# Unpaired last lags of a mixed-scale convolution: one stacked stationary and a 64-row product in place of two 128-row products

## The reference

```
x = x + L0(_gn(x), ...)      # mixture of experts: 8 experts, top 2
x = x + L1(_gn(x), ...)      # three layers of this kind, L1 to L3
x = x + L2(_gn(x), ...)
x = x + L3(_gn(x), ...)

def _L1_conv_ref(x, w3, w7, w15, w_mix):          # 4 batches, 512 tokens, 16 heads of 32
    x_flat = x.reshape(b, l, h * d).transpose(0, 2, 1)
    outs = [_causal_dwconv(x_flat, w) for w in (w3, w7, w15)]   # causal, one filter per channel
    y = jnp.concatenate(outs, axis=1)
    y = y.reshape(b, h, n_scales * d, l).transpose(0, 3, 1, 2)
    return jnp.einsum('blhm,dm->blhd', y, w_mix)
```

## Time and profile before

| | us |
|---|---|
| median of 3 runs (1032.67 to 1033.59) | 1032.7 |
| the profiled execution, whole | 1034.63 |
| its span, first to last instruction | 1033.0 |
| PE busy in the span | 992.5 (96%) |
| DVE busy | 498.2 (48%) |
| ACT busy | 323.2 (31%) |
| POOL busy | 255.8 (25%) |

### The profile page before, as it was taken

How to read it: one execution, slowest core, us unless ns; L and a number is a source line. 1 busy time by engine, 2 the same in 40 slices (tenths; PEclk the granted TensorE clock), 3 DMA queues, 4 the chain that set the end, 5 groups by cost and what they waited for, 6 DMA issues and landing times.

```text
span 1033.0 us, 14467 instructions
## 1 busy us (share of the span) xinstructions
PE 992.5 (96%) x5077; PEld 829.1 (80%) x5078; DVE 498.2 (48%) x660; ACT 323.2 (31%) x437; POOL 255.8 (25%) x359
## 2 busy tenths in 40 slices
PE   4989999999999999999999999968999999999998
PEld 3568888888888888888887888857988898889787
DVE  6763263145136246116337155146733896489411
ACT  2613252144144144125235244122511222122223
POOL 1011112121112112111212111112534245424531
PEclk9999999999999999999999999998999999999999
DMA  9576118934971994981893994975467747674668
GB/s 371 234 263 206 22 30 334 392 107 180 393 259 28 397 393 128 409 303 28 335 389 129 396 376 138 406 222 169 143 204 169 219 143 203 165 223 144 192 152 226
DMA packets 98786, 238.12 MB, mean 231 GB/s; under 512 B 10048, under 2 KB 64576, under 8 KB 83840
## 3 DMA queue, kind: packets, MB, share of 16 engines
q1 hardware_dynamic: 90528, 214.54, 57.6%
q0 software_dynamic: 8080, 23.07, 9.5%
q10 hardware_dynamic: 144, 0.07, 0.0%
HBM read 129.91 MB, written 111.94 MB: 234 GB/s over the span
## 4 chain that ended last, share of the span: by engine, by line
PE 75%; DMA 8%; DVE 6%; issue 5%; SPq 4%; ACT 1%; POOL 0%; ACTq 0%; DVEq 0%; POOLq 0%
PE gate_ps L1020 15%; PE up_ps L1020 15%; PE y_ps L1007 10%; PE head_ps L1598 6%; PE head_ps L1594 6%; PE head_ps L1595 6%; PE y_ps L1010 5%; DMA w_raw<-in_w13T 4%; PE hT_ps L1032 2%; SPq L460 2%; DMA ring<-filters 1%; PE xT_ps L997 1%; DMA rowed<-acc 1%; PE head_ps L1613 1%; PE head_ps L1614 1%
## 5 line engine op out<-in xcount | busy, mean ns | idle before, releaser
L1020 PE MATMUL gate_ps<-front 128*128 128x512 f32 x560 | 176.4, 396 | 2.2 <-DVE xT_lo L867 1.5
L1020 PE MATMUL up_ps<-front 128*128 128x512 f32 x560 | 173.2, 390 | 0.0
L1594 PE MATMUL head_ps<-split,ring 128*128 128x256 f32 (+1 forms) x459 | 158.9, 346 | 4.0 <-DMA ring<-filters 2.4
L1598 PE MATMUL head_ps<-split,ring 128*128 128x256 f32 (+1 forms) x459 | 155.3, 338 | 2.2 <-DVE split L1396 2.2
L1595 PE MATMUL head_ps<-split,ring 128*128 128x256 f32 (+1 forms) x459 | 153.8, 335 | 0.0
L882 DVE TENSOR_TENSOR hidden<-silu,up_ps 128x1024 f32<-128x1024 f32 x35 | 42.7, 1221 | 228.7 <-ACT silu L641 228.7
L1020 PEld LDWEIGHTS up_ps<-front 128*128 128x128 f32 x560 | 105.4, 188 | 22.3
L1020 PEld LDWEIGHTS gate_ps<-front 128*128 128x128 f32 x560 | 102.6, 189 | 22.8 <-DVE front L831 1.8
L528 POOL DMA_INDIRECT acc<-y_row,put x35 | 67.4, 1927 | 214.4 <-ACT y_row L629 214.4
L641 ACT ACTIVATE silu<-gate_ps 128x1024 f32<-128x1024 f32 x35 | 35.9, 1024 | 267.5 <-PE up_ps L1020 267.5
L1007 PE MATMUL y_ps<-w_hi,hT_hi 128*128 128x512 f32 x280 | 112.2, 401 | 1.2 <-ACT hT_hi L623 1.2
(11 more groups left out here) (198 smaller groups left out, 1435.1 us busy)
## 6 DMA issues: line engine op xcount, KB each, us to landing
filters<-rows SPq DMA_DIRECT2D x56, 1568.0 KB
w_raw<-in_w13T SPq DMA_DIRECT2D x32, 1024.0 KB, 16.4
ring<-filters SPq DMA_DIRECT2D x15, 1536.0 KB, 6.6
w_raw<-in_w2T SPq DMA_DIRECT2D x16, 1024.0 KB, 6.0
ring<-filters SPq DMA_DIRECT2D x144, 64.0 KB, 4.1
ring<-filters SPq DMA_DIRECT2D x12, 768.0 KB, 4.8
ring<-filters SPq DMA_DIRECT2D x15, 384.0 KB, 3.7
ring<-filters SPq DMA_DIRECT2D x9, 512.0 KB, 4.0
```

The costliest lines, as they stand in the source:

```text
L1020: last = nc.tensor.matmul(o[:, n, :], a[:, k, :], b[:, k, t, n * 512:(n + 1) * 512], start=(k == 0 and a is xT_hi and b is w13_hi), stop=( ...
L1594: nc.tensor.matmul(place, kernel_hi, x_hi, start=(u == 0 and a == 0), stop=False)
L1598: nc.tensor.matmul(place, kernel_hi, x_lo, start=False, stop=False)
```

## The change

The parts are stored and stacked the other way round, and the unpaired unit is computed from one stacked stationary matrix:

- `filter_sb` has the low part at index 0 and the high part at index 1, and so has DRAM. `at_block` moves by `LAGS` elements so that it lies over the half that is not cleared.
- The unpaired unit's filters come by one transfer: low in rows 0 to 63, high in rows 64 to 127. Three transfers become one. The two transfers of the paired windows now carry one part each for both units, 128 rows of 512 bytes instead of 64 rows of two parts.
- `single` holds x high in both halves; `tail` waits for `high_ok` only.
- PE computes high filter by low x as a product of 64 rows (64 to 127) straight from `split`, behind a wait for `low_ok`, and then one 128-row product of the stacked matrix with `single`. Two matmuls remain two.

```diff
@@ RING_COUNT
-    RING_COUNT.append((_l + 1) * (len(head_runs(_h)) + 5))
+    RING_COUNT.append((_l + 1) * (len(head_runs(_h)) + 3))
@@ experts_part
-        at_block = late_rows[:, 0:TOP_K * TILES * COLUMNS].rearrange(...)
+        at_block = late_rows[:, LAGS:LAGS + TOP_K * TILES * COLUMNS].rearrange(...)
-                        nc.scalar.activation(filter_sb[:, i, 0].bitcast(f32r), filter_sb[:, i, 1], ACT.Copy)...
+                        nc.scalar.activation(filter_sb[:, i, 1].bitcast(f32r), filter_sb[:, i, 0], ACT.Copy)...
-                    nc.vector.tensor_tensor(filter_sb[:, i, 1].bitcast(f32r), filter_sb[:, i, 1], filter_sb[:, i, 0],
+                    nc.vector.tensor_tensor(filter_sb[:, i, 0].bitcast(f32r), filter_sb[:, i, 0], filter_sb[:, i, 1],
                                             ALU.subtract).then_inc(filter_ok, 1)
@@ load_filters
-                for half, m in zip((1, 0), head_shared(h)):
-                    s, j, count = head_parts(h)[m]
-                    begin = SCALE_AT[s] + count * P
-                    sp.dma_start(ring[half * P // 2:(half + 1) * P // 2, at:at + 2 * P].bitcast(f32).rearrange("p (a n) -> p a n", n=P),
-                                 filter_rows[P // 2:P, 2 * (l * GROUPS + j):2 * (l * GROUPS + j + 1), begin:begin + P]).then_inc(ring_in[h], 16)
+                m = head_shared(h)[0]
+                s, j, count = head_parts(h)[m]
+                begin = SCALE_AT[s] + count * P
+                for part in range(2):
+                    sp.dma_start(ring[:, at + part * P:at + (part + 1) * P].bitcast(f32),
+                                 filter_rows[P // 2:P, 2 * (l * GROUPS + j) + part:2 * (l * GROUPS + j) + part + 3:2, begin:begin + P]
+                                 .rearrange("r u n -> u r n")).then_inc(ring_in[h], 16)
                 at += 2 * P
                 s, j, count = head_parts(h)[head_single(h)]
                 begin = SCALE_AT[s] + count * P
-                sp.dma_start(ring[:, at + P:at + 2 * P].bitcast(f32), filter_rows[:, 2 * (l * GROUPS + j) + 1, begin:begin + P]).then_inc(ring_in[h], 16)
-                for half in range(2):
-                    sp.dma_start(ring[half * P // 2:(half + 1) * P // 2, at:at + P].bitcast(f32),
-                                 filter_rows[P // 2:P, 2 * (l * GROUPS + j), begin:begin + P]).then_inc(ring_in[h], 16)
+                sp.dma_start(ring[:, at:at + P].bitcast(f32),
+                             filter_rows[P // 2:P, 2 * (l * GROUPS + j):2 * (l * GROUPS + j + 1), begin:begin + P].rearrange("r s n -> s r n")).then_inc(ring_in[h], 16)
@@ tail, on POOL
-                pool.wait_ge(low_ok, piece)
                 nc.gpsimd.tensor_copy(moving(single[0:P // 2, at], pair, 0),
-                                      moving(split[P // 2:P, j, 1], pair, 0).bitcast(f32)).then_inc(single_ok, 1)
+                                      moving(split[P // 2:P, j, 0], pair, 0).bitcast(f32)).then_inc(single_ok, 1)
@@ head, on PE
-                kernel_hi, kernel_lo = (ring[:, (2 * at + part) * P:(2 * at + part + 1) * P] for part in range(2))
-                x_both = moving(single[:, SINGLE_SLOT[h]], pair, a)
+                j = head_units(h)[head_single(h)][1]
+                kernel_both = ring[:, 2 * at * P:(2 * at + 1) * P]
+                pe.wait_ge(low_ok, l * len(PIECES) + PIECE_OF[j, pair] + 1)
+                nc.tensor.matmul(place, kernel_both[P // 2:P, :], moving(split[P // 2:P, j, 1], pair, a), start=False, stop=False)
                 pe.wait_ge(single_ok, 2 * (n + 1))
-                nc.tensor.matmul(place, kernel_hi, x_both, start=False, stop=False)
-                last = nc.tensor.matmul(place, kernel_lo, x_both, start=False, stop=True)
+                last = nc.tensor.matmul(place, kernel_both, moving(single[:, SINGLE_SLOT[h]], pair, a), start=False, stop=True)
                 last.then_inc(head_done, 1)
```

More of the change, by code:

```diff
@@ L296, in experts_part @@
             "p (j i c) -> p j i c", j=TOP_K, i=TILES)
-        at_block = late_rows[:, 0:TOP_K * TILES * COLUMNS].rearrange("p (j i c) -> p j i c", j=TOP_K, i=TILES)
+        at_block = late_rows[:, LAGS:LAGS + TOP_K * TILES * COLUMNS].rearrange("p (j i c) -> p j i c", j=TOP_K, i=TILES)
         weight_block = w2_lo[:, :, :].rearrange("p k n -> p (k n)")[:, TOP_K * TILES * COLUMNS:(1 + PARTS_OF_WEIGHT) * TOP_K * TILES * COLUMNS].rearrange(
@@ L612, in after_first @@
                         act.wait_ge(product_ok, e * 2 + (i - 1))
-                        nc.scalar.activation(filter_sb[:, i, 0].bitcast(f32r), filter_sb[:, i, 1], ACT.Copy).then_inc(filter_hi_ok, 1)
+                        nc.scalar.activation(filter_sb[:, i, 1].bitcast(f32r), filter_sb[:, i, 0], ACT.Copy).then_inc(filter_hi_ok, 1)
             def xT_high(g):
@@ L648, in _ @@
             for i in range(2):
-                nc.scalar.activation(filter_sb[:, i, 1].rearrange("p (a d) -> p a d", d=HD),
+                nc.scalar.activation(filter_sb[:, i, 0].rearrange("p (a d) -> p a d", d=HD),
                                      lasting.whole[:, None, 0:HD].to_broadcast([P, LAGS // HD, HD]), ACT.Copy, scale=0.0).then_inc(filter_zero, 1)
@@ L853, in after_first @@
                         last = nc.vector.tensor_tensor(
-                            filter_sb[:, i, 1, at:at + k * HD].rearrange("p (k d) -> p k d", d=HD),
+                            filter_sb[:, i, 0, at:at + k * HD].rearrange("p (k d) -> p k d", d=HD),
                             taps_sb[:, c, tap:tap + k].rearrange("p o k -> p (o k)")[:, :, None].to_broadcast([P, k, HD]),
@@ L1233, in share @@
                     pool.wait_ge(head_done, slot_free(l, i))
-                for half, j in ((1, 2 * tile), (0, 2 * tile + 1)):
+                for half, j in ((0, 2 * tile), (1, 2 * tile + 1)):
                     nc.gpsimd.tensor_copy(both_parts(shared[half * P // 2:(half + 1) * P // 2, slot], pair),
@@ L1588, in head @@
                     for a in range(count):
-                        kernel_hi, kernel_lo = (ring[:, (2 * at + part * count + a) * P:(2 * at + part * count + a + 1) * P]
+                        kernel_lo, kernel_hi = (ring[:, (2 * at + part * count + a) * P:(2 * at + part * count + a + 1) * P]
                                                 for part in range(2))
@@ L1601, in head @@
                 a = head_parts(h)[head_shared(h)[0]][2]
-                kernel_hi, kernel_lo = (ring[:, (2 * at + part) * P:(2 * at + part + 1) * P] for part in range(2))
+                kernel_lo, kernel_hi = (ring[:, (2 * at + part) * P:(2 * at + part + 1) * P] for part in range(2))
                 x_hi, x_lo = (moving(shared[:, TILE_SLOT[head_tile(h)], part], pair, a) for part in range(2))
```

## The result

The changed kernel takes 1131.85 us (median of 4 runs, 1130.42 to 1134.53) beside 1032.68 for the kernel before: ratio 1.0963, 95% interval 1.0939 to 1.0988. That is 99 us slower. The forecast was 1050.6 with a range of 1028 to 1056: slower it is, but by more than five times as much as forecast (99.2 for 17.9), and far outside the range.

What follows compares the result with a forecast made beforehand. PE was taken as the bound; +23.8 for shape changes, -2.0 absorbed, -0.2 POOL, -2.8 transfers, -0.9 layer start gave +17.9 on 1032.7, so 1050.6 us. The 8-in-10 range was 1028 to 1056.

Steps and rivals of the forecast that it cites:

- PE is the bound, and an added cost on it counts nearly in full: Whole kernel: PE busy 992.5 of 1033.0 us, so added PE cost counts almost in full wherever heads run.
- The absorption: Transitions between layers: PE's existing waits for DVE and other stops absorb part of the added cost, -2.0 us (0 to -4).
- The change of shape: PE, 66 tasks: 132 changes between 128-row and 64-row stationary matrices at 0.18 us each, +23.8 us, upper bound 26.4.
- Rivals 1 and 2: PE's row changes: free, 1028.8 us (0.27 together with rival 4), or half price, 132 x 0.07, 1037.5 us (0.13).
- the pull-ahead of weights: PE: weight loads going to the background buffer are pulled ahead, so 64-row weights load beside a running 128-row product.
- rival 1: PE: no price for the change of rows; sum -3.9, 1028.8 us, faster; chance 0.27 together with rival 4.
- Rival 4: PE: 64-row product runs as 128 rows with idle rows, no shape change; time of rival 1; chance 0.27 together.
- SP and the transfers: SP queue: 96 issues and 3 MB less, paired transfers costed the same; PE's four ring waits go, -2.8 us.
- The start of the layers: Rows of batches 2 and 3 issued 1.3 to 2.1 us sooner, shortening DVE's wait: -0.9 us (0 to -0.9).
- POOL, the new wait for low_ok, the exchange of halves: POOL's last copy delays PE less, -0.2 us; PE's added wait is already over, nothing; swapping filter halves, nothing.
- The ring waits of before: PE's four waits for filters, 2.4 us, all go because two issues less a head bring the last forward 1.1 us.
- The signs: Traces expected: own 64-row shape, later weight loads, lower PE busy share, no ring waits, batch rows issued before 696.5.

Runs made afterwards that it cites:

- e1: The changed kernel with its part-window transfers put back to 64 rows each, four a head instead of three, the 64-row product kept: 1056.34 us, ratio 1.0217.
- e3: The changed kernel with both edits, transfers of 64 rows each and a 128-row product in place of the 64-row one: 1032.00 us, ratio 0.9989.
- e7: The kernel of e1 with the 64-row product issued twice in a row: 1067.09 us.
- e2: The changed kernel, its three transfers untouched, with high filter by low x as a product of all 128 rows: 1121.32 us, ratio 1.0855.
- e4: The kernel of e1 with the two paired transfers again in the changed form (outer dimension 2): 1077.25 us.
- e5: The kernel of e1 with the unpaired stack by the change's one transfer (outer dimension 2): 1055.37 us.

## Why the prediction was wrong, by its steps

- **PE is the bound, and an added cost on it counts nearly in full.** Right for the kernel with transfers of 64 rows: 24.3 us (e1 - e3) for 23.8 - 2.0 = 21.8. The absorption is there too: between the profiled executions of e3 and e1 PE's records are 27.9 us longer (991.7 and 1019.6) and its idle time is 3.3 shorter (38.3 and 35.0). Of the 27.9, up to 3 us are not the change itself but a lower clock: from 720 to 730 it is 0.71 in e1 and 1.00 in e3. The forecast did not have that term.
- **The change of shape.** The mechanism was right and its size near: 0.09 + 0.10 us a change in e7 for 0.07 to 0.09 + 0.11. A change of columns was a good row for a change of rows. The extra time lies elsewhere than forecast: spread over three distances (0.33, 0.42, 0.34 with 512 columns) where two of about 0.41 were named. The Trainium skill (TensorEngine Tiling (Array Packing), Key Properties) says that a change of the tiling mode drains the engine; the trace agrees, with 0.09 us in front of each product of a new shape. That the 64 rows themselves cost nothing more is shown by e7 alone. Rivals 1 and 2 and the pull-ahead of weights that rival 1 leaned on fall for this case: the loader stood idle for 0.37 and 0.24 us. Rival 4 falls by the shape `64*128` in the records.
- **SP and the transfers: the step that failed.** "The two paired transfers keep their bytes and their 512-byte pieces, so I cost them the same", and the three-in-one as a plain saving. Bytes, pieces and issues are not all that a transfer is: its outer dimension went from 64 or 128 to 2, and with it, by the packet counts, the engines from 16 to 2. The term was taken as -2.8 us; it measured +75.5 (changed - e1), or +89.3 without the 64-row product (e2 - e3). No transfer of that form ran before, so it should have been bounded. An estimate, once one knows of the two engines: 16 heads a layer need filters every 6.7 us (107/16). 192 packets on each of two engines are 98 KB. At half of the 44 GB/s above that is 4.5 us; with a sixteenth of the 409 GB/s that the page of before has at most, 3.8 us. The full windows come in series, as the row of GB/s shows: 896 KB a head on the mean, at 370 GB/s 2.5 us. 6.3 to 7.0 us of transfer for 6.7 us of products leaves nothing to catch up with.
- **The start of the layers.** Costed -0.9, it came out about +2.0: DVE waited 0.92 us for these rows before and 2.90 in the changed kernel, where it began at 708.83 instead of 705.97. (The rest of that distance is a shift of the whole: the first head starts at 701.72 instead of 700.91.) The same failed step: two issues of line 1183 and one of 1189 took 7.2 us of SP. In e3, with one issue less than before, the rows went out at 696.18 and DVE began at 704.80. But the first head also starts 0.7 us earlier there, and DVE's wait is 0.87 us. So hardly any of the -0.9 shows where the transfers are good.
- **POOL, the new wait for low_ok, the exchange of halves.** Right: none shows a cost; e3 holds them all and takes 1032.0.
- **The ring waits of before.** In e3 PE has none left, with one issue less a head, which fits the reason given (fewer issues); no run parts that from the fewer bytes. But the median fell by only 1 to 2 us, less than the 3.9 of rival 1's sum.
- **The signs.** The 64-row shape and the later weight loads came as named. PE's busy share did not fall in e1 (97% for 96%), since the records around a change get longer, with no gap. In the changed kernel the ring is PE's largest wait instead of gone, and the rows of batches 2 and 3 go out at 701.46 instead of before 696.5.
- **The range.** Built from the doubt about PE alone. Nothing in it stood for a transfer that gets slower. The right direction was in part luck: the larger cost by far was one that the forecast did not have.

What stays open in part: how much of the 75.5 us is the lower clock behind long waits and how much the waits themselves. No run parts the two, but the traces of e1 and of the changed kernel (spans 1054.6 and 1131.2) bound them. PE waits 45.0 us more for the ring, and its records are 28.1 us longer in sum (1019.6 and 1047.7), which is the most that the lower clock can add inside them. At least some 14 us of it are that clock, by an estimate: from 709 us on, 193 full products of the heads in the changed kernel and 75 in e1 stand at the distances of the 1.2 GHz level (0.21 and 0.43 us).

## What to carry to other kernels

When a diff rearranges a transfer, look at the outermost dimension of both its sides, not only at bytes, pieces and issues: a stack of two written as one transfer can sit on two of sixteen engines. Two transfers of 64 rows were then better than one of 2 x 64 once there were two or three such transfers a head (e4 and the changed kernel against e1), and no worse with one (e5). The count of small packets on the page is a check on the number of engines. On PE, one product with another number of rows among full ones pays about 0.19 us on the way in and as much on the way back; where the operands allow it, a full product that adds a harmless term is cheaper (e3: 24 us less than e1). Its extra rows add a term as small as the ones that the kernel leaves out.

## What the runs showed of the hardware that was not expected

- On each of two engines 64 packets a head cost nothing that shows, 128 cost 21 us, 192 cost 75.5: the price begins before the transfers of a head fill the time of its products (by the estimate above 128 packets take 3.0 us, with the full windows 5.5 of 6.7).
- Slow transfers slow the issues behind them on the same engine: the untouched issue of line 1176 went from a median of 0.43 to 1.46 us, and is back at 0.37 in e1.
- The price of a change of shape has two nearly equal parts, 0.09 and 0.10 us, that stand apart when two products of the new shape follow each other (e7).
